# Attention B, tiles 0 to 3: a score bank per head, k turned and split ahead of q, and the output product's second half behind the turning

## The reference

```python
q = _dequant_matmul(hidden_states, qw_q, scales_q)   # 32 heads
k = _dequant_matmul(hidden_states, qw_k, scales_k)   # 8 heads
v = _dequant_matmul(hidden_states, qw_v, scales_v)
q = _apply_rope(q, cos, sin)
k = _apply_rope(k, cos, sin)
scores = jnp.einsum('bhqd,bhkd->bhqk', q, k) / math.sqrt(HD)
scores = jnp.where(causal[None, None], scores, jnp.finfo(scores.dtype).min)
attn = jax.nn.softmax(scores.astype(jnp.float32), axis=-1)
ctx = jnp.einsum('bhqk,bhkd->bhqd', attn, v)
return _dequant_matmul(ctx, qw_o, scales_o)
```

## Time and profile before

| | |
|---|---|
| median of three runs | 1515.82 us (1514.83 to 1516.57) |
| profiled execution | 1517.17 us, span 1515.4 us, mean granted clock of TensorE 0.995 |
| PE busy | 1447.4 us (96%), 8164 matmuls |
| DVE busy | 1228.2 us (81%) |
| ACT busy | 874.5 us (58%) |
| POOL busy | 253.0 us (17%) |
| attention B | from about 583 to 1470 us, a group about 109 us |

### The profile page before, as it was taken

The page is one execution under the profiler, slowest core; times in us unless marked ns, Lnnn a source line. Parts: engine busy times, 40 slices in busy tenths (PEclk is TensorE's granted clock), DMA queues, the critical chain, the costliest instruction groups (busy, mean ns, idle before and its releaser), DMA issues.

```text
span 1515.4 us, 24024 instructions
## 1 busy us (share of the span) xinstructions
PE 1447.4 (96%) x8164; PEld 720.0 (48%) x8164; DVE 1228.2 (81%) x2578; ACT 874.5 (58%) x1474; POOL 253.0 (17%) x193
## 2 busy tenths in 40 slices
PE   5999999999999997999999999999999999999898
PEld 3453333333332454555555555555555555555454
DVE  3698888888884587888898888887988888878954
ACT  2247777777678134665665665665665655756631
POOL 3312000000000222212212212212212212111011
PEclk8999999999999999999999999999999999999999
DMA  3894000000001253576675675675674675643541
GB/s 100 146 139 132 1 0 0 0 0 0 0 1 20 57 139 93 121 152 136 129 143 133 126 150 132 128 150 125 135 160 107 135 153 121 137 93 71 99 74 56
DMA packets 351757, 143.70 MB, mean 95 GB/s; under 512 B 314680, under 2 KB 324408, under 8 KB 351648
## 3 DMA queue, kind: packets, MB, share of 16 engines
q1 hardware_dynamic: 351664, 142.50, 44.9%
HBM read 58.66 MB, written 6.19 MB: 43 GB/s over the span
## 4 chain that ended last, share of the span: by engine, by line
PE 76%; DVE 15%; ACT 5%; issue 3%; DMA 0%; SPq 0%; DVEq 0%; ACTq 0%
PE ps L1597 10%; PE ps L1599 10%; PE ps L1598 10%; PE ps L1352 8%; PE ps L1405 8%; PE ps L1391 7%; PE ps L1556 4%; PE ps L1678 3%; PE ps L1680 3%; PE ps L1679 3%; DVE mx L899 2%; DVE nmr L1101 2%; PE ps L1519 2%; PE ps L1284 2%; DVE hl L1118 2%
## 5 line engine op out<-in xcount | busy, mean ns | idle before, releaser
L729 ACT ACTIVATE x<-ps,nmb,factor 128x128 f32<-128x128 f32 (+7 forms) x256 | 211.4, 831 | 289.1 <-DVE nmb L1103 289.1
L899 DVE TENSOR_REDUCE mx<-ps 128x1 f32<-128x512 f32 x512 | 326.9, 686 | 50.5 <-PE ps L1352 48.3
L637 ACT ACTIVATE proj<-ps 128x1024 f32<-128x1024 f32 x256 | 248.3, 1021 | 98.5 <-PE ps L1391 97.6
L1118 DVE SCALAR_TENSOR_TENSOR hl<-x,rden,hl 128x128 f16<-128x128 f32 (+7 forms) x256 | 208.1, 813 | 8.9 <-ACT hl L737 8.4
L737 ACT ACTIVATE hl<-x,rden 128x128 f16<-128x128 f32 (+7 forms) x256 | 184.1, 767 | 25.2 <-DVE rden L1114 24.4
L1101 DVE TENSOR_REDUCE nmr<-ps 128x1 f32<-128x128 f32 (+7 forms) x256 | 191.9, 750 | 3.3 <-PE ps L1661 2.4
L534 POOL TENSOR_TENSOR tmp<-tmp 128x640 f32<-128x640 f32 x64 | 98.5, 1539 | 514.4 <-DVE tmp L1097 514.4
L1352 PE MATMUL ps<-ks,qs 96*128 (+1 forms) x512 | 181.3, 383 | 2.4 <-DVE mx L899 1.0
L1597 PE MATMUL ps<-wh,xTh 128*128 128x256 f16 (+1 forms) x512 | 166.8, 326 | 0.0
L1598 PE MATMUL ps<-wl,xTh 128*128 128x256 f16 (+1 forms) x512 | 166.8, 326 | 0.0
L1599 PE MATMUL ps<-wh,xTl 128*128 128x256 f16 (+1 forms) x512 | 166.8, 326 | 0.0
(11 more groups left out here) (173 smaller groups left out, 2199.2 us busy)
## 6 DMA issues: line engine op xcount, KB each, us to landing
scale<-sp_n SPq DMA_DIRECT2D x32, 384.0 KB, 4.4
st<-in_L_attn_b_qw_q_dram SPq DMA_DIRECT2D x32, 256.0 KB, 2.8
st<-in_L_attn_b_qw_o_dram SPq DMA_DIRECT2D x32, 256.0 KB, 2.9
scale<-so_n SPq DMA_DIRECT2D x32, 256.0 KB, 3.5
qs<-scratch SPq DMA_DIRECT2D x18, 256.0 KB, 9.4
hlT<-hl SPq DMA_TRANSPOSE x256, 3.4
scratch<-pieces SPq DMA_DIRECT2D x5, 768.0 KB, 8.6
xnat<-attn_a_hidden_state_dram SPq DMA_DIRECT2D x8, 256.0 KB, 5.1
```

Of the source, the lines that this page charges most:

```text
L637: nc.scalar.activation(pbuf[:, e % 4, :].rearrange("p (b n) -> p b n", b=2), ps[:, b:b + 2, :], ACT.Exp, scale=float(HD) ** -0.5).then_inc ...
L729: nc.scalar.activation(pr[:, h, 0:n], flat(2 * (h % 2), n), ACT.Exp, bias=nmb[:, h:h + 1], scale=factor[:, par, 0:1], accum_out=den[:, h:h ...
L899: nc.vector.tensor_reduce(mx[:, f, k // 2, k % 2:k % 2 + 1], ps[:, bank(k), :], AX.X, ALU.max).then_inc(s_mx, 1)
L1118: nc.vector.scalar_tensor_tensor(hl[:, h, n:2 * n], pr[:, h, 0:n], rden[:, h:h + 1], hl[:, h, 0:n], ALU.mult, ALU.subtract).then_inc(s_lo, 1)
```

## The change

Four things, all in attention B. (1) `score_bank`: in steps 0 to 3, where scores fit in one bank, each head has its own (0, 2, 1, 3), so keys don't wait for an exponential of the same step there; in steps 1 to 3 they wait for the same head's exponential of the step before, in step 0 those of heads 0 and 1 as before. (2) k is turned ahead of q, with a semaphore of its own; ACT and DVE take k's parts first; DVE's low part of q comes in two halves of two heads, and keys 0 wait for k and the first half alone. This is so in every step. (3) In steps 1 to 3 `output_second` stands behind the turning, and ahead of keys 3, in its place, the values of heads 0 and 1 of tile `one`; ACT's `high_part` in these steps stands behind `turned`. (4) `keep_busy` in group 0: in steps 0 and 1 two of 512 columns behind keys 3, one more behind the turning of step 0, in place of 512 and 256 ahead of keys 3 in both and one of 512 ahead of step 1; they write bank 4 and not 3.

```diff
--- before.py
+++ after.py
@@ -224,6 +224,10 @@
         def v_slot(t, par):
 
             return t if t > 1 else t + T * par
+
+        def score_bank(t, h):
+
+            return (0, 2, 1, 3)[h] if t < T // 2 else 2 * (h % 2)
 
         def k_slot(t, par):
 
@@ -314,6 +318,7 @@
         s_rpa = sem("s_rpa")
         s_vl = sem("s_v_lo")
         s_vb = sem("s_vb")
+        s_kT = sem("s_k_turned")
         s_qkT = sem("s_qkT")
         s_qke = sem("s_qke")
         s_sc = sem("s_sc")
@@ -698,11 +703,12 @@
                                      scale=HEADROOM / (XSCALE * WSCALE)).then_inc(s_vb, 1)
 
             def turned(v, t, par):
+                c = k_slot(t, par) * P
+                act.wait_ge(s_kT, v + 1)
+                nc.scalar.activation(kTh[:, c:c + P], ps[:, 7, 0:P], ACT.Copy,
+                                     scale=HEADROOM / (XSCALE * WSCALE)).then_inc(s_qke, 1)
                 act.wait_ge(s_qkT, v + 1)
                 nc.scalar.activation(qTh[:, t % 2].rearrange("p h n -> p (h n)"), ps[:, 6, :], ACT.Copy,
-                                     scale=HEADROOM / (XSCALE * WSCALE)).then_inc(s_qke, 1)
-                c = k_slot(t, par) * P
-                nc.scalar.activation(kTh[:, c:c + P], ps[:, 7, 0:P], ACT.Copy,
                                      scale=HEADROOM / (XSCALE * WSCALE)).then_inc(s_qke, 1)
 
             def context_high(g, t):
@@ -726,7 +732,7 @@
                         act.wait_ge(s_nat[h], 64)
                         act.wait_ge(s_xh, 2 * T + 2 * h + 2)
                     act.wait_ge(s_nb, u * R + h + 1)
-                    nc.scalar.activation(pr[:, h, 0:n], flat(2 * (h % 2), n), ACT.Exp, bias=nmb[:, h:h + 1],
+                    nc.scalar.activation(pr[:, h, 0:n], flat(score_bank(t, h), n), ACT.Exp, bias=nmb[:, h:h + 1],
                                          scale=factor[:, par, 0:1], accum_out=den[:, h:h + 1]).then_inc(s_eb, 1)
 
                 def high(h):
@@ -753,9 +759,11 @@
                 values(u + 1, par if t < T - 1 else 1 - par, t2)
                 high(0)
                 high(1)
-                if not last:
+                if not last and not 1 <= t <= 3:
                     high_part(g + 1, t, 1 - par)
                 turned(u + 1, t2, par if t < T - 1 else 1 - par)
+                if not last and 1 <= t <= 3:
+                    high_part(g + 1, t, 1 - par)
                 exponentials(2)
                 exponentials(3)
                 if exists(*before(g, t, 1)):
@@ -1098,7 +1106,7 @@
 
             def maximum(u, h, n, par):
                 dve.wait_ge(s_sc, u * R + h + 1)
-                nc.vector.tensor_reduce(nmr[:, h:h + 1], flat(2 * (h % 2), n), AX.X, ALU.max, negate=True).then_inc(s_mxb, 1)
+                nc.vector.tensor_reduce(nmr[:, h:h + 1], flat(score_bank(n // P - 1, h), n), AX.X, ALU.max, negate=True).then_inc(s_mxb, 1)
                 dve.wait_ge(s_mxb, u * R + h + 1)
                 nc.vector.tensor_scalar(nmb[:, h:h + 1], nmr[:, h:h + 1], factor[:, par, 0:1], None,
                                         ALU.mult).then_inc(s_nb, 1)
@@ -1120,13 +1128,16 @@
 
             def turned(v, t, par):
 
-                dve.wait_ge(s_qke, v * 2 + 2)
-                nc.vector.scalar_tensor_tensor(qTl[:, t % 2].rearrange("p h n -> p (h n)"), ps[:, 6, :],
-                                               HEADROOM / (XSCALE * WSCALE), qTh[:, t % 2].rearrange("p h n -> p (h n)"),
-                                               ALU.mult, ALU.subtract).then_inc(s_ql, 1)
                 c = slice(k_slot(t, par) * P, (k_slot(t, par) + 1) * P)
+                dve.wait_ge(s_qke, v * 2 + 1)
                 nc.vector.scalar_tensor_tensor(kTl[:, c], ps[:, 7, 0:P], HEADROOM / (XSCALE * WSCALE), kTh[:, c],
                                                ALU.mult, ALU.subtract).then_inc(s_ql, 1)
+                dve.wait_ge(s_qke, v * 2 + 2)
+                for h in range(0, R, 2):
+                    nc.vector.scalar_tensor_tensor(qTl[:, t % 2, h:h + 2, :].rearrange("p h n -> p (h n)"),
+                                                   ps[:, 6, h * P:(h + 2) * P], HEADROOM / (XSCALE * WSCALE),
+                                                   qTh[:, t % 2, h:h + 2, :].rearrange("p h n -> p (h n)"),
+                                                   ALU.mult, ALU.subtract).then_inc(s_ql, 1)
 
             def add(v, t, par):
                 dve.wait_ge(s_op, v + 1)
@@ -1257,7 +1268,7 @@
                     elif phase == 2 and t >= 2:
                         pe.wait_ge(s_xl, t - 1)
                     elif phase == 3 and t < 2:
-                        pe.wait_ge(s_ql, G * T * 2)
+                        pe.wait_ge(s_ql, G * T * 3)
                     elif phase == 3 and t in (4, 5):
                         pe.wait_ge(s_eb, G * T * R)
                     for k in range(KC):
@@ -1617,9 +1628,9 @@
             def turn_b(v):
                 pe.wait_ge(s_rpa, v + 1)
                 pe.wait_ge(s_vl, v + 1)
-                for h in range(BH):
-                    dst = ps[:, 6, h * P:(h + 1) * P] if h < R else ps[:, 7, 0:P]
-                    ins = nc.tensor.transpose(dst, rc1[:, h * P:(h + 1) * P], ident[:])
+                nc.tensor.transpose(ps[:, 7, 0:P], rc1[:, R * P:BH * P], ident[:]).then_inc(s_kT, 1)
+                for h in range(R):
+                    ins = nc.tensor.transpose(ps[:, 6, h * P:(h + 1) * P], rc1[:, h * P:(h + 1) * P], ident[:])
                 ins.then_inc(s_qkT, 1)
 
             def output(v, heads, par):
@@ -1645,11 +1656,13 @@
             def keys(g, t, h, par):
                 u = g * T + t
                 n = (t + 1) * P
-                if h >= 2:
+                if 1 <= t < T // 2:
+                    pe.wait_ge(s_eb, u * R + h + 1 - R)
+                elif h < 2 and exists(*before(g, t, 1)):
                     pe.wait_ge(s_eb, u * R + h - 1)
-                elif exists(*before(g, t, 1)):
+                elif h >= 2 and t >= T // 2:
                     pe.wait_ge(s_eb, u * R + h - 1)
-                b = 2 * (h % 2)
+                b = score_bank(t, h)
                 for c in range(0, n, 512):
                     w = min(512, n - c)
                     at = c + (k_slot(t, par) * P if par else 0)
@@ -1687,10 +1700,9 @@
                 last = isinstance(g, int) and g == G - 1
                 end = last and t == T - 1
                 one, two = before(g, t, 1), before(g, t, 2)
-                if g == 0 and t == 1:
-                    keep_busy(3, wbT, 512)
-                pe.wait_ge(s_ql, u * 2 + 2)
+                pe.wait_ge(s_ql, u * 3 + 2)
                 keys(g, t, 0, par)
+                pe.wait_ge(s_ql, u * 3 + 3)
                 if not end:
                     project_all(u + 1, *after(g, t), par if t < T - 1 else 1 - par)
                 keys(g, t, 1, par)
@@ -1699,19 +1711,24 @@
                 keys(g, t, 2, par)
                 if end:
                     tokens(3, 0, 1)
-                if exists(*two):
+                if exists(*two) and not 1 <= t <= 3:
                     output_second(*two, par if t >= 2 else 1 - par)
+                early = R // 2 if t < T // 2 and exists(*one) else 0
+                if early:
+                    values(*one, par if t >= 1 else 1 - par, 0, early)
+                keys(g, t, 3, par)
                 if g == 0 and t <= 1:
-                    keep_busy(3, wbT, 512)
-                    keep_busy(3, wbT, 256)
-                early = R // 2 if t == 0 and exists(*one) else 0
-                if early:
-                    values(*one, 1 - par, 0, early)
-                keys(g, t, 3, par)
+                    pe.wait_ge(s_xl, T)
+                    for _ in range(2):
+                        keep_busy(4, wbT, 512)
                 if not end:
                     turn_b(u + 1)
+                    if g == 0 and t == 0:
+                        keep_busy(4, wbT, 512)
                 else:
                     tokens(3, 2, 3)
+                if exists(*two) and 1 <= t <= 3:
+                    output_second(*two, par if t >= 2 else 1 - par)
                 if exists(*one):
                     values(*one, par if t >= 1 else 1 - par, early, R)
```

## The result

The changed kernel took 1518.85 us (median of 17 runs, 1517.37 to 1522.28), the kernel before 1515.12 (17 runs, 1513.78 to 1517.22): a ratio of 1.0025, 95% interval 1.0018 to 1.0032. The forecast was 1509.3 and its range ended at 1515.5, so the sign was wrong too. The profiled execution took 1520.92 us.

A forecast was written before the change was run, and what follows sets the result against it. PE's waits before keys 0, some 29 us in all, were the ceiling, with DVE nearly as full; 1.73 + 6 x 0.70 + 0.6 = 6.5 us gained gave 1509.3 us, range 1502 to 1515.5.

The forecast's parts named there:

- POOL and SP* issue what they did: Attention B: POOL and SP issue the same work; the weight's low part starts 0.7 us later on an idle POOL.
- Turning held by `vl` at 817.02: Third group: PE still starts turning at 817.17; waits on `vl` of about 1.2, 0.8 and 0.5 us in steps 1 to 3.
- A half of `qTl` at 0.33: DVE: each half of q's low part takes 0.33 us, by a line between two rows; bounds 0.20 and 0.61.
- 1.73 for group 0: Group 0 gains 1.46 us by earlier keys 0 in steps 1 and 2, plus 0.08 and 0.19 in the last steps.
- 6 x 0.70: PE's lead into step 4, 0.51 + 0.19 = 0.70 us, is kept in each of six groups.
- 0.6 for group 7: Group 7 has no dequantising or high part, so PE's own order decides: about 0.6 us gained.
- The clock: PE's granted clock in group 0 stays at 1.00 (2.4 GHz) despite 1.6 us of idle in one piece in step 0.
- DVE gains 0.43 in step 1, PE 0.79: Third group, step 1: DVE reaches the cosine product 0.43 us earlier, and PE starts keys 0 0.79 us earlier.
- 1: Rival: PE's waits vanish without heirs, all 29 us go, 1487 us, or half of it, 1501; chance 0.08.
- 2: Rival: the last transposes, in step 0, eat the lead, 0.4 to 0.8 us a group lost, 1513.8 us; chance 0.14.
- 3: Rival: PE's clock falls once in group 0, 1513.2 us; chance 0.05.
- 4: Rival: exponentials 2 and 3 come late behind the high part if `kTh` starts by 818.1; +10 us, 1526; chance 0.08.

The follow-up runs named there:

- experiment 4: Changed kernel with the weight's high part right behind exponential 0 on ACT and POOL's low part ahead of rope's sum, in steps 1 to 3: 1507.23 us, 0.9944.
- experiment 2: Changed kernel with POOL's low part of the weight in steps 1 to 3 replaced by a memset of the same tile: 1507.55 us, 0.995.
- experiment 5: Kernel before plus the banks, k ahead of q and halves of q's low part; output product, values and high part unmoved: 1509.63 us, 0.996.
- experiment 1: Changed kernel with ACT's high part of the weight back ahead of the turned tiles in steps 1 to 3: 1509.47 us, 0.9959.
- experiment 9: Experiment 4 with PE's old order, the output product where it stood before the change: 1506.8 us, 0.9946.
- experiment 7: Experiment 4 with `vh` ahead of exponential 1 on ACT and `vl` ahead of the first inversion on DVE: 1505.7 us, 0.993.
- experiment 10: Experiment 7 with PE's old order, the output product where it stood before the change: 1501.28 us, 0.9904.

## Why the prediction was wrong

**The step that failed** is "*POOL and SP* issue what they did. The low part starts 0.7 later on a POOL that is idle". It looked at POOL's queue for what the delay costs and not at DVE, which reads and writes the same memory: the later start (0.69, as forecast) put it on top of low 1 in three steps of each of seven groups. It was the one term costed at nothing whose cover I did not name. It could be seen coming: the prediction has low 1 from about 819.35 to 819.8 and the high part from 818.43, and POOL began 0.90 behind it (818.58 above, and 817.68), so from 819.33 to 820.97. The size could be seen too. Low 1 began 0.23 us ahead of POOL's end before the change, took 0.51 for 0.47, and ended 0.28 behind POOL (820.50 and 820.22). Put behind 820.97 by as much, low 1 is done at 821.25, and the inversion is some 0.8 late against 820.38 (measured 0.74). That is at most 21 x 0.8 = 17 us against 6.5 of gain; the stage paid 12.9. This was the rival on the slower side to have named.

The Trainium skill, "SBUF — State Buffer", section "Who interferes with whom", states the mechanism: a VectorE instruction with two inputs in SBUF contends with a GpSimd instruction that reads SBUF, not with one that only writes it, and who comes second is blocked until the other is done. By this rule the change should be slower at these 21 places, and the runs agree: low 1 (inputs `x` and `hl`) 1.92 us beside a reading POOL, 0.47 beside a memset; `qTl` and `kTl` (one input in PSUM) were not held up before the change (0.69 and 0.28 us, with POOL's row beside them or not). The 0.67 of the inversion in experiment 4 agrees with its further rule that a `tensor_scalar` can take both port pairs, though no run here isolates that.

**What held**, in experiment 2, where the collision is out:
- Turning held by `vl` at 817.02: right in size, 1.21, 0.76 and 0.42.
- A half of `qTl` at 0.33: the pair starts at 818.62 and low 1 behind it at 819.28 in the changed kernel.
- The sum. Forecast: 1.73 for group 0, 6 x 0.70, 0.6 for group 7. By the cosine products group 0 went from 107.64 to 106.02 (1.62), groups 1 to 6 from 652.66 to 647.15 (5.51), group 7 from 75.71 to 75.33 (0.38): 7.5 us against 6.5, and 7.9 by the medians. Most of the excess lies in groups 4 and 5, where before lost 0.9 and 0.6 more than in the others and the new version does not. Group 7 gave less than its 0.6; in PE's old order (experiment 5) it takes 75.04 and gives 0.67.
- The clock: 1.00 in all windows shown, and in 583 to 592 us of the changed kernel.

**What was right for less than it said.** "DVE gains 0.43 in step 1, PE 0.79": DVE's 0.43 decides, and it comes from k ahead of q. Experiment 5 has it without moving the output product (step 1 takes 10.95 for 11.41, 0.46 less). I had written that PE keeps what DVE lets it keep, and did not draw from it that PE's part of the change was then worth nothing. It is worth nothing in sum, and not in every group. Step 0 takes 12.02 us where nothing is late. Before, it took 12.89, 12.62 and 12.35 in groups 4, 5 and 6, and in experiment 5 12.59, 12.31 and 12.02. In the moved order (experiment 1) it takes 12.02 in groups 4 and 5, but 12.27 and 12.49 in groups 2 and 6.

**The rivals.** 1: no, the waits on `vl` took their place. 2: no, its waits got shorter in sum (1.3 us before in three groups, 0.4 after in two). 3: no, the granted clock stayed at 1.00. 4 had the sign, but not the cause: `kTh` started at 817.61, before its limit of 818.1, and exponential 3 was read when forecast.

## What to carry to other kernels

Moving an instruction moves what follows it on other engines: for each of them, write down what runs at the new time on the engine that it can hold up, also when its own queue is empty. Here long elementwise work of GpSimd cost nothing beside VectorE instructions that took an input from PSUM. And where two engines are nearly full, find out which one's step paces the loop before reordering the other: here two orders of TensorE, in three pairs of kernels (experiments 1 and 5, 4 and 9, 7 and 10), gave the same mean time of a group to 0.05 us.

## What was unexpected in the hardware

- A VectorE instruction held up by POOL shows as **busy**, with no idle time and no releaser: 1.92 us for 0.47 of work. A comparison of the same form in two places (means of 791 and 475 ns) or POOL's row beside it reveals it; the page's share of busy DVE went up, as if there were more work.
- It is held whole, not slowed in proportion. Low 1 ended 0.28 or 0.29 us behind POOL's low part in step 1, 0.41 or 0.42 in step 2 and 0.54 or 0.55 in step 3, in each of the seven kernels in which it started inside it, and whether it had started 1.6 us or 0.2 us ahead of POOL's end. That is 0.2 less than its own 0.47, 0.61 and 0.74.
- Small size is no protection: an inversion of 128x2 took 0.67 to 0.92 us for 0.16 beside POOL's sum of rope (experiments 4, 7, 9 and 10). The factor product of one column (`nmb`, 128x1) took 0.21 or 0.22 beside POOL and elsewhere.
- A memset of the same tile on POOL, 0.74 us from 0.02 ahead of low 1, held up nothing.
